# One-core mLSTM and mixture-of-experts block: log decay contracted over 128 rows, expert rows folded on GpSimd

## The reference

```
xn = layernorm(x)
q, k, v = headwise 4x4 blocks of wq, wk, wv applied to xn        # 4 heads of 32
ig, fg  = gates of xn, one per head and token
log_D[s, t] = cumsum(log_sigmoid(fg)) differences + ig[t], lower triangle only
D = exp(log_D - row max);  C = (q k^T / sqrt(32)) * D
h = (C / max(|row sum of C|, exp(-row max))) v, then layernorm per head, times (1 + ln_w)
top1 = argmax(softmax(xn router_w + router_b))
y = (a * sigmoid(g)) w2[top1] + b2[top1],  (a, g) = xn w1[top1] + b1[top1]
out = x + h * silu(y)
```

## Time and profile before

| | us |
|---|---|
| median of 3 runs | 250.81 |
| lowest and highest | 248.66, 251.05 |
| the profiled execution | 249.57 |
| its span | 247.5 |

### The profile page before, as it was taken

How to read it: one execution, slowest core, us unless ns; L and a number is a source line. 1 busy time by engine, 2 the same in 40 slices (tenths; PEclk the granted TensorE clock), 3 DMA queues, 4 the chain that set the end, 5 groups by cost and what they waited for, 6 DMA issues and landing times.

```text
span 247.5 us, 5928 instructions
## 1 busy us (share of the span) xinstructions
PE 211.2 (85%) x1811; PEld 172.4 (70%) x1819; DVE 178.7 (72%) x474; ACT 124.4 (50%) x287; POOL 103.3 (42%) x127
## 2 busy tenths in 40 slices
PE   0788878598999889977999998999999999999730
PEld 0677743244565555647999998999999999996400
DVE  3987297645658869865877978797889888672390
ACT  1179577135555455547555654655565556640120
POOL 7526602344445446520043346334643454466060
PEclk9979999659999999999999999999999999999996
DMA  6799992282013799532001293201120210000794
GB/s 172 215 201 153 250 415 81 58 213 102 28 45 107 219 247 255 198 98 56 0 33 56 56 317 83 61 22 52 49 62 20 53 54 33 17 21 11 217 316 146
DMA packets 37756, 29.67 MB, mean 120 GB/s; under 512 B 3419, under 2 KB 34403, under 8 KB 37725
## 3 DMA queue, kind: packets, MB, share of 16 engines
q1 hardware_dynamic: 34286, 24.98, 39.3%
q0 software_dynamic: 2272, 4.22, 4.9%
q10 hardware_dynamic: 1168, 0.10, 0.3%
HBM read 20.20 MB, written 9.54 MB: 120 GB/s over the span
## 4 chain that ended last, share of the span: by engine, by line
PE 69%; issue 7%; DMA 6%; DVE 5%; ACT 5%; POOL 1%; ACTq 1%; SPq 1%; DVEq 1%; POOLq 0%
PE bank L1128 12%; PE bank L1137 12%; PE head_bank L1128 12%; PE bank L1075 7%; PE bank L1055 5%; PE head_bank L1065 5%; PE bank L1086 4%; PE head_bank L976 3%; PE bank L1054 3%; DMA nat<-in_L_attn_wk 2%; DMA xw<-y_tokens 2%; PE bank L961 2%; PE head_bank L1041 2%; PE bank L952 1%; DVE ra L641 1%
## 5 line engine op out<-in xcount | busy, mean ns | idle before, releaser
L450 POOL DMA_INDIRECT y_tokens<-ffn,xs_sb x39 | 38.9, 997 | 72.8 <-DVE ffn L924 71.9
L445 POOL DMA_INDIRECT xs_sorted<-xw,pos x32 | 31.6, 988 | 35.2 <-PE head_bank L1065 23.3
L1137 PE MATMUL bank<-w_sb,dm 128*128 x312 | 41.4, 276 | 1.2 <-DVE dm L908 1.2
L1137 PEld LDWEIGHTS bank<-w_sb,dm 128*128 128x128 f32 x312 | 38.0, 192 | 1.6 <-issue 1.6
L1128 PE MATMUL bank<-xsT,wc 128*128 128x128 f32 x320 | 39.1, 275 | 0.0
L1128 PEld LDWEIGHTS bank<-xsT,wc 128*128 128x128 f32 x320 | 37.3, 192 | 0.0
L1128 PE MATMUL head_bank<-xsT,wc 128*128 128x128 f32 x304 | 37.0, 275 | 0.0
L805 DVE TENSOR_TENSOR cm<-dm,head_bank 128x1024 f32<-128x1024 f32 (+1 forms) x32 | 29.1, 949 | 10.3 <-PE head_bank L1065 8.9
L1128 PEld LDWEIGHTS head_bank<-xsT,wc 128*128 128x128 f32 x304 | 35.4, 192 | 0.0
L563 ACT ACTIVATE dm<-bank 128x512 f32<-128x512 f32 x48 | 26.9, 596 | 15.8 <-PE bank L1055 12.9
L586 ACT ACTIVATE wc<-w_sb 128x512 f32 x39 | 24.6, 630 | 15.1 <-issue 15.1
(11 more groups left out here) (187 smaller groups left out, 347.4 us busy)
## 6 DMA issues: line engine op xcount, KB each, us to landing
w_sb<-in_L_ffn_w SPq DMA_DIRECT2D x12, 512.0 KB, 12.4
x_sb<-in_L_attn_x SPq DMA_DIRECT2D x16, 256.0 KB, 4.9
wc<-in_L_ffn_w SPq DMA_DIRECT2D x8, 512.0 KB
xs_sorted<-pad_row SPq DMA_DIRECT2D x1, 2515.5 KB, 23.5
xs_sb<-xs_sorted SPq DMA_DIRECT2D x13, 193.5 KB, 2.7
xw<-y_tokens SPq DMA_DIRECT2D x8, 256.0 KB, 4.5
out_x<-xw SPq DMA_DIRECT2D x8, 256.0 KB, 3.2
y_tokens<-ffn,xs_sb POOLq DMA_INDIRECT x39
```

What stands on the lines that cost most here:

```text
L445: pool.indirect_dma_start(xs_dram, bass.IndirectOffsetOnAxis(ap=pos[:, t:t + 1], axis=0), xw[:, t, :], None).then_inc(s_scat, 16)
L450: pool.indirect_dma_start(y_dram, bass.IndirectOffsetOnAxis(ap=xs_sb[:, j // CH % NX, j % CH, D:DW].bitcast(I32), axis=0), ys_sb[:, j // C ...
L1137: last = pe.matmul(bank[6 + j % 2][:, 0:D], uT[:, j % 2, c, :], w2_sb[:, bass.ds(e * (HC * D) + c * D, D)], start=(c == 0), stop=(c == HC ...
```

## The change

`left` gets a column block for every batch, [128, 16, 256], four times as large. GpSimd fills it with zeros. VectorE then writes ones into four blocks of 32 rows and 1024 columns, one for each strip, between its last `evac_vl` and the gate inputs, after a wait for GpSimd's fill. SP waits for these four before it loads `left`. The indicator is limited to the first 12 rows of each strip. The decay of batches 0 to 3 is contracted over rows 0 to 14 as before, that of batches 4 to 15 over all 128 rows, and batch 4 waits for the loads of all strips. The folds go from VectorE to GpSimd, one behind every fourth scatter.

```
-        left = sb("left", [P, NBS, S], BF16)
+        left = sb("left", [P, B, S], BF16)
...
             sp.wait_ge(s_left, 2)
+            sp.wait_ge(s_lone, 4)
...
-                sp.dma_start(left[32 * i:32 * i + 3 * NH, :, :],
+                sp.dma_start(left[32 * i:32 * i + 3 * NH, NBS * i:NBS * (i + 1), :],
...
-            pool.memset(left[:, :, :], 1.0).then_inc(s_left, 1)
+            pool.memset(left[:, :, :], 0.0).then_inc(s_left, 1)
...
+                if t % 4 == 3:
+                    e = t // 4
+                    if e == 0:
+                        pool.wait_ge(s_w1, 16 * E)
+                    pool.wait_ge(s_bc[e % 3], 16 * (e // 3 + 1))
+                    pool.tensor_tensor(w1_sb[0:P - 1, e, :], w1_sb[0:P - 1, e, :], last_row[0:P - 1, e % 3, :],
+                                       ALU.subtract).then_inc(s_sub, 1)
...
-            dve.tensor_reduce(ind[:, :], ident[:, :].rearrange("p (g h) -> p h g", h=NH), AX.X, ALU.add).then_inc(s_ind, 1)
+            dve.tensor_reduce(ind[:, :], ident[:, :].rearrange("p (i g h) -> p h i g", i=4, h=NH)[:, :, :, 0:3], AX.XY, ALU.add).then_inc(s_ind, 1)
...
             evac_vl(9)
+            dve.wait_ge(s_left, 1)
+            for i in range(4):
+                dve.memset(left[32 * i:32 * (i + 1), NBS * i:NBS * (i + 1), :], 1.0).then_inc(s_lone, 1)
             dve.wait_ge(s_vla, NV - len(DVE_VL))
...
-                    if 6 <= b < 6 + E:
-                        fold_row(b - 6)
...
-                rows = slice(32 * i, 32 * i + 3 * NH + 3)
+                rows = slice(0, 3 * NH + 3) if i == 0 else slice(0, P)
...
-                pe.matmul(bank[n % 2][:, :], left[rows, j, s0:s0 + P], right[rows, :, j, t0:t0 + P],
+                pe.matmul(bank[n % 2][:, :], left[rows, b, s0:s0 + P], right[rows, :, j, t0:t0 + P],
```

More of the change, by code:

```diff
@@ L242, in mlstm_moe_block @@
         s_dummy = sem("s_dummy")
+        s_lone = sem("s_lone")
         s_y0 = sem("s_y0")
@@ L823, in attention @@
                 copy_w(0)
[L825 to L830, removed]
             def normalise(g):
@@ L1050, in log_decay @@
                     pe.wait_ge(s_dm, n - 1)
-                if j == 0 and m == 0:
-                    pe.wait_ge(s_lr[i], 32)
+                if n == 0:
+                    pe.wait_ge(s_lr[0], 32)
+                if i == 1 and j == 0 and m == 0:
+                    for strip in range(1, 4):
+                        pe.wait_ge(s_lr[strip], 32)
                 if m != 1:
                     pe.matmul(bank[n % 2][:, :], ident_bf[:, :], maskn[:, :, :].rearrange("p h t -> p (h t)"), start=True, stop=False)
-                pe.matmul(bank[n % 2][:, :], left[rows, j, s0:s0 + P], right[rows, :, j, t0:t0 + P],
+                pe.matmul(bank[n % 2][:, :], left[rows, b, s0:s0 + P], right[rows, :, j, t0:t0 + P],
                           start=(m == 1), stop=True).then_inc(s_ld, 1)
```

## The result

| | before | change |
|---|---|---|
| median of 4 runs, us | 250.34 | 264.4 |
| lowest and highest | 248.66, 251.05 | 263.41, 265.47 |
| the profiled execution's span | 247.5 | 262.8 |

The ratio is 1.0573, with an interval of 1.0503 to 1.0643. The change is 14 us slower. I had forecast 255.0 and a range to 258.6: the sign was right, the size was not.

What follows compares the result with a forecast made beforehand. Bound by the start's chain through VectorE's gate inputs and the attention's TensorE-ScalarE loop; 4.2 + 2.35 - 1.4 = +5.15 on the profiled 249.57 gave 254.7, put at 255.0 us, range 251.3 to 258.6.

Steps and rivals of the forecast that it cites:

- steps 3 to 5: Attention's end: gain of 2.1 us from folds off VectorE and decays, cut to 1.4 by GpSimd's slower queue.
- the longer half clock of the attention: Start of attention: its half-clock stretch was left as it is, with no cost; 3 us back if it went away.
- 1, the fills: Start, VectorE ahead of the gate inputs: four fills delay them, +4.2 us, bounds +1.1 and +4.2.
- Rival A: Start: fills are cheap, below 0.6 us each, and the clock may hold; not slower, 249.3 us; 15%.
- 2, the clock: Start, TensorE's sums to counts: longer idle time brings 1.2 GHz, +2.35 us, bounds 0 and 5.2.
- Rival B: Start: fills cost 4.2 us but TensorE's clock stays at 2.4 GHz; +2.8, 252.4 us; 17%.
- steps 1 and 2: Start: the fills' delay of 4.2 us and the half clock's 2.35 us, both losses.
- 3, the folds off VectorE: Attention batches: taking eight folds of 1.22 us off VectorE gains at most 1.48 us.
- 4, the decays: Attention, 12 batches: 128-row decays change a batch by -0.08 to +0.02 us, taken as -0.05, in all -0.6.
- Rival D: Attention: steps of shape stay and scores lose their company, decays cost 12 x 0.22 = +2.6 us; 257.2 us; 7%.
- 5, the folds on GpSimd: Attention, GpSimd: four scatters and a fold take 7.55 us against 7.33 for two batches, cutting the 2.1 gain to 1.4.
- Rival C: Attention's end: a fold takes 3.0 us instead of 2.4, GpSimd's queue turns the gain into +2.8; 258.9 us; 5%.

Runs made afterwards that it cites:

- e2: Kernel before plus only the four VectorE fills of ones, with SP waiting for them, on chip 14: 252.85 us, ratio 1.0197.
- e5: Kernel before with 128-row decays for batches 4 to 15, GpSimd filling zeros and ones after its copy of the indicator, folds on VectorE, chip 12: 248.13 us, 1.0076.
- g0: The change as it is, run again as control on chip 1: 264.13 us, ratio 1.0525.
- e0: The change as it is, run again on chip 12: 253.62 us, ratio 1.0289.
- g1: The change with its folds back on VectorE (batches 6 to 13), fills and 128-row decays kept, chip 1: 259.10 us, ratio 1.0316.
- f0: The kernel before, run again for a trace on chip 1: 251.18 us, ratio 1.002.
- f3: Kernel before with six calls of products of zeros on TensorE ahead of the first decay, chip 1: 247.78 us, ratio 0.9818.
- g3: Kernel before with four calls of products of zeros on TensorE ahead of the first decay, chip 1: 248.18 us, ratio 0.9848.
- e3: Kernel before with only the folds moved to GpSimd, one behind every fourth scatter, chip 14: 248.53 us, ratio 1.0053.
- f4: Kernel before with only the folds moved to GpSimd, one behind every third scatter, chip 1: 257.40 us, ratio 1.0225.
- f2: The change plus products of zeros on TensorE, 12 calls ahead of the gates' sums and 5 ahead of the first decay, chip 1: 261.57 us, ratio 1.0398.
- g2: The change with second expert weights and bias loaded only behind the first load of sorted rows, chip 1: 271.77 us; ratio of lowest three runs 1.0711.
- e4: Kernel before with 128-row decays, GpSimd filling zeros and ones ahead of its copy of the indicator, folds on VectorE, chip 14: 255.84 us, 1.0293.

## Why the prediction was wrong, step by step
Two terms of the sum failed. The one that decides is the -1.4 for the folds and decays (steps 3 to 5): the result's last twelve batches and what follows up to the first expert product took 4.3 us more and not 1.4 less. With that number in its place the sum is 249.57 + 6.55 + 4.3 = 260.4, above my range. The other is the longer half clock of the attention, which I had put at nothing and which is +3.6. Put right alone it gives 254.7 + 3.6 = 258.3, still inside.

**1, the fills: right.** I took +4.2, and the gate inputs are 4.3 later against the last value copy. One fill takes 0.91 us for 1024 elements, and 1.18 from start to start (I had 1.14). The Trainium skill (VectorE: DVE Perf Modes, "Zero memsets can be issued as uint32 (trn2)") has a memset at a cycle an element whatever its type, from which the prediction estimated 4.3 us for the four. The trace is near it: 4.44 us from the first start to the last end. One fill by itself takes 0.89 ns an element, and 1.15 with the gap behind it; only bf16 was filled, so that the type does not matter is not shown. Rival A is out. `e2` shows that these fills alone make the start 5.7 us longer, and `e5` that the start is whole without them.

**2, the clock: right in the sums, missed in the attention.** Sums to counts took 6.82 us instead of 5.17, +1.65 against my +2.35. The stretch of 36.5 to 43.3 covers 3.3 us of them, and half of that is 1.65. In `g0` it covers 5.9 us (39.6 to 45.5) and costs 2.9. The size depends on where the stretch falls, and my 4.7 us of cover lay between. Rival B is out. The sum of steps 1 and 2, +6.55, stands beside +5.9 measured, and +7.2 in `g0`.

What I said of the attention's own half clock, "I leave it as it is", was right of chip 12 (10.2 us in `e0`) and of `g1` (10.2), and wrong of the result (20.5) and of `g0` (17). This was +3.6 and +2.0 in the first three batches, against the first trace of the kernel before; against `f0`, on the same chip as `g0`, the +2.0 is gone (16.16 and 16.32 us). The pause before the first decay did not grow: it was 2.77 us and is 2.41 in the result and 1.83 in `g0`. The cause of the longer stretches is open: `f0` shows 17 us in the kernel before, so they don't need the change. `f3` and `g3` show what the stretch of 10.2 us in the first trace is worth, 3.6 us in the first three batches (10.57 instead of 14.21), and against the 17 us of `f0` it is 5.75.

**3, the folds off VectorE: nothing.** I had up to 1.48 us, the difference between batches with and without folds. On chips 12 and 14 the batches take 3.48 us with folds on VectorE (`e2`) and without (`e3`). A fold of 1.2 us lies in VectorE's idle time. On chip 1 the batches of `g1` with folds take 3.48 to 4.09 us. Some of that may be the folds, but no run on this chip is without them and without GpSimd's.

**4, the decays: right on chips 12 and 14 within what can be measured.** I took -0.05 us a batch, and it is between 0.00 (by the two batches above) and +0.02 (41.71 us for twelve batches in `e2`, 41.92 in `e5`): the two gaps of 0.10 that go, and the start of the scores that moves 0.31 back, seem to cancel. (By its runs `e5` is 1.65 us over the kernel before; its trace shows 0.3 of that in the start and 0.2 in the twelve batches.) Rival D, at +0.22 a batch, is out there. On chip 1 the three batches from the fifth scores on, ahead of any fold on VectorE, take 3.75 us each in `g1` and 3.64 to 3.67 in `f0`, which would be +0.1 for the decays; but the first two of them take 3.51 and 3.48 in `g0`, which has the same decays. No run on this chip has the decays alone, so it is open there.

**5, the folds on GpSimd: this is the step that failed.** Its timing held: a fold takes 2.37 us, and a group of four scatters and a fold about 7.5. The timeline of GpSimd at the end of the attention, as in the earlier trace rows:

```profile
121.67 0.96 POOL L447 DMA_INDIRECT xs_sorted<-xw,pos  x1 [0.31 <-issue]
122.65 2.38 POOL L454 TENSOR_TENSOR w_sb<-w_sb,wc 127x1024 f32<-127x1024 f32 x1
```

Where nothing holds the batches up, as in `e0`, GpSimd's backlog costs 0.8 us behind the last scores. So without any further effect steps 3 to 5 are +0.8 and not -1.4, and the change is at +7.1 on chip 12. That lies inside the upper end of my range (+8.3 over the median before), but with a term of the wrong sign, so it is no success of the mechanism. In the result steps 3 to 5 are another thing: ScalarE stands for 4.65 us (one to three times 3 to 4.7 us in the traces of chip 1) and waits for something that the trace can't name, then TensorE runs at half clock. `g0` less `g1` puts that at 5.0 us (by the medians), `f4` less the kernel before, without any other part of the change, at 6.0. The 5.0 can hold some luck of the clock: in the two traces the last twelve batches differ by 5.2 us, but the start and the first three batches by another 3.5, by where the half clock lay. No term and no rival had it. Rival C looked at the same place, GpSimd's queue, but for a longer fold, and the fold did not get longer. (Its working has a slip: the seven groups are counted from 54.7, where the sentence before has 54.3. The 0.4 us change nothing here.)

**The whole.** In the medians of chip 1 the change costs 12.8 us: 7.8 for the fills, their clock and the decays (`g1`), 5.0 for the folds on GpSimd. The result has 1.2 us more (14.06). Its first three batches are 1.6 us longer than those of `g0`, but its start and its last twelve batches are 1.2 and 1.5 us shorter, so these stages do not explain the 1.2.

**What stays open** is the mechanism of these waits. They come with GpSimd's folds (the result, `f2`, `f4`, `g0`, `g2` and not `f0`, `f3`, `g1`, `g3`, all but the first on chip 1), they don't come on chips 12 and 14 with the same program, and they are not the second weights (`g2`). The five longest (4.3 to 4.7 us of idle time, in the result, `f2`, `g0` and twice in `g2`) begin behind the start of the first scatter after a fold, by 1.1 us in three of them and 1.5 in two, and all five end 0.95 to 1.02 us behind the start of the next fold: they last about as long as GpSimd issues its four scatters. That was seen in traces, and no experiment moved a scatter against a batch to test it. Nor does any run tell whether it is the fold's own work on GpSimd or the way it bunches the scatters.

## What to carry to other kernels
An operation put ahead of a chain that other engines wait for is paid twice, once by its length and once by the clock that TensorE loses while it idles: four fills of 0.9 us made the start 5.7 us longer by themselves, and 5.7 to 7.2 within the change. The reverse was the best thing found: 2 to 3 us of products of zeros in TensorE's idle time ahead of the attention gave 1.5 to 1.8%, on the one chip where it was tried. Work that lies in the idle time of an engine (the folds on VectorE) has no price until the trace shows what waits for it, and moving it to the engine that issues the scatters brought a new one. And before moving GpSimd's work in time, look at what VectorE reads then.

## What the runs showed of the hardware that I had not expected
- GpSimd's copy of 3.6 us out of SBUF held four small VectorE additions with two SBUF operands for 3.4 us (4.07 instead of 0.67, and 4.21 in `e4`), and not when it ran 7 us earlier.
- The same program runs at another pace on another chip. Fourth to sixteenth scores take 41.7 to 41.9 us in eight traces on chips 12 and 14, and 45.0 to 45.5 in the traces of the kernel before and its warmed forms on chip 1 and in the first one. A part of it is ScalarE's wait ahead of the copy of the values sum. The groups of that copy from 75 to 100 us, in `e2` (chip 14) and in `f0` (chip 1), with the idle time behind the bar:

```profile
L572 ACT ACTIVATE uTs<-bank 128x256 f32<-128x256 f32 x7 | 2.7, 383 | 6.2 <-PE bank L1080 5.3 <-issue 0.9
```

```profile
L570 ACT ACTIVATE uTs<-bank 128x256 f32<-128x256 f32 x7 | 2.7, 384 | 8.4 <-PE bank L1075 8.4
```

  It is 0.87 to 0.93 us each time on chip 14, and on chip 1 either 0.8 to 1.0 or 1.5 to 1.7. On chip 12 it is 1.08 us in most batches of `e0`, and they take 3.48 us all the same, so this wait is not all of it. A difference of that size between two chips says nothing of a change.
- 1.99 us of products and then 0.68 us of idle time before the first decay left the clock at 2.4 GHz (`g3`), where 2.77 us of idle time did not.
